# A dense weighted aggregation on TensorE: weight passes in one sweep on both column halves of the array, with four buffers of 3125 columns each loaded in one transfer

## The reference

```
x = _layernorm(x + _L2_gnn_ref(x, src, dst, edge_weight, gamma))

def hgcn_forward(x, rows, cols, edge_weight, gamma):     # rows = src, cols = dst
    h = x
    for _ in range(2):                                   # NUM_LAYERS
        msg = edge_weight[:, None] * h[cols]
        h = segment_sum(msg, rows, num_segments=6250)    # h = A h, A[row, col] = sum of weights
        h = proj(h)
        h = h * (1.0 / sqrt(|mink(h, h)|))
        h = lorentz_batchnorm(h, gamma)                  # means over all nodes, log map, exp map
    return h
```

## Time and profile before

| | |
|---|---|
| Runs | 7061.76, 7067.46, 7078.11 us; median 7067.46 |
| Profiled execution | 7070.5 us, of which the span (first to last record) is 7068.7 us |
| PE busy | 5556.2 us (79% of the span) |
| DVE / ACT / POOL busy | 3231.5 / 1350.6 / 2157.1 us |
| First weight pass | from 5516 to 6048 us |
| Second weight pass | from 6127 to 6659 us |

### The profile page before, as it was taken

The page is one execution under the profiler, slowest core; times in us unless marked ns, Lnnn a source line. Parts: engine busy times, 40 slices in busy tenths (PEclk is TensorE's granted clock), DMA queues, the critical chain, the costliest instruction groups (busy, mean ns, idle before and its releaser), DMA issues.

```text
span 7068.7 us, 161419 instructions
## 1 busy us (share of the span) xinstructions
PE 5556.2 (79%) x52264; PEld 4488.9 (64%) x52265; DVE 3231.5 (46%) x5888; ACT 1350.6 (19%) x3492; POOL 2157.1 (31%) x3521
## 2 busy tenths in 40 slices
PE   0999988877777779988377777777777899599765
PEld 0777777666666679988376777777666444244365
DVE  7999888777777740122333333333333100300233
ACT  0122234455555520000111111111111000100100
POOL 1222222222222210000377777777776000000000
PEclk9999999999999989998555555555565899799887
DMA  1011123334434339885533333333333799499565
GB/s 35 21 54 54 61 90 100 111 121 137 128 127 138 125 139 388 347 339 221 113 79 76 76 77 78 76 76 79 76 76 72 244 300 305 164 305 298 194 260 203
DMA packets 427400, 1053.65 MB, mean 149 GB/s; under 512 B 126711, under 2 KB 283713, under 8 KB 398401
## 3 DMA queue, kind: packets, MB, share of 16 engines
q1 hardware_dynamic: 377090, 1000.81, 42.4%
q0 software_dynamic: 50176, 51.48, 4.0%
HBM read 809.69 MB, written 242.41 MB: 149 GB/s over the span
## 4 chain that ended last, share of the span: by engine, by line
PE 49%; POOL 15%; DVE 14%; issue 10%; DMA 4%; ACT 3%; POOLq 2%; ACTq 2%; DVEq 0%; SPq 0%; PEldq 0%; PEld 0%
PE banks L1496 16%; POOL WORK L599 15%; PE banks L1526 15%; PE banks L1457 11%; PE banks L1488 4%; DVE T L803 3%; DMA WORK<-table,idx 3%; DVE T L810 2%; ACTq L332 1%; POOLq L336 1%; DVE WORK L879 1%; DVE WORK L892 1%; ACT WORK L1310 1%; DMA T<-qtable 1%; ACT ACC L1255 1%
## 5 line engine op out<-in xcount | busy, mean ns | idle before, releaser
L599 POOL DMA_INDIRECT WORK<-table,idx x1568 | 1525.9, 973 | 1372.1 <-DVE idx L898 894.3
L1496 PE MATMUL banks<-T 128*128 128x125 bf16 (+1 forms) x21696 | 1672.8, 226 | 41.4 <-DVE T L810 8.0
L1496 PEld LDWEIGHTS banks<-T 128*128 128x128 bf16 x21696 | 1446.4, 115 | 337.0 <-DVE T L810 321.3
L803 DVE TENSOR_TENSOR T<-T 128x750 bf16<-128x750 bf16 x1808 | 1001.6, 554 | 394.3 <-PE banks L1496 308.6
L556 POOL TENSOR_TENSOR T<-T 128x12 f32 x1816 | 551.0, 303 | 1785.1 <-DVE T L810 1289.7
L1526 PE MATMUL banks<-T,WORK 125*64 125x400 f32 (+1 forms) x3200 | 1056.6, 493 | 45.4 <-ACT WORK L1325 41.5
L810 DVE TENSOR_TENSOR T<-T 128x750 bf16<-128x750 bf16 x1808 | 1001.0, 554 | 62.1
L1488 PE MATMUL banks<-T 128*128 128x250 bf16 x3616 | 711.8, 278 | 364.4 <-DVE T L803 125.2
L1457 PE MATMUL banks<-WORK,T 125*128 125x192 bf16 (+1 forms) x10000 | 833.1, 247 | 63.1 <-DVE WORK L942 63.1
L1457 PEld LDWEIGHTS banks<-WORK,T 125*128 125x128 bf16 (+1 forms) x10000 | 830.9, 99 | 65.3 <-issue 59.3
L1526 PEld LDWEIGHTS banks<-T,WORK 125*64 125x64 f32 x3200 | 439.9, 138 | 661.5 <-issue 619.0
(11 more groups left out here) (337 smaller groups left out, 3428.1 us busy)
## 6 DMA issues: line engine op xcount, KB each, us to landing
T<-dense_c SPq DMA_DIRECT2D x200, 1562.5 KB, 8.3
T<-dense_w SPq DMA_DIRECT2D x300, 800.0 KB, 4.2
dense_w<-WORK SPq DMA_DIRECT2D x250, 546.9 KB
T<-dense_w SPq DMA_DIRECT2D x100, 725.0 KB, 4.1
WORK<-rel_rows SPq DMA_DIRECT2D x197, 256.0 KB, 4.0
WORK<-in_eaT SPq DMA_DIRECT2D x196, 256.0 KB
dense_c<-T SPq DMA_DIRECT2D x13, 3125.0 KB, 10.6
dense_c<-ACC SPq DMA_DIRECT2D x12, 3125.0 KB, 10.7
```

Of the source, the lines that this page charges most:

```text
L599: nc.gpsimd.indirect_dma_start(out=g_sb[:, u, c * D:(c + 1) * D], out_offset=None, in_=table, in_offset=bass.IndirectOffsetOnAxis(ap=idx[: ...
L803: V.tensor_tensor(planes[:, v, 0:HOTS].rearrange("p (k n t) -> p k n t", k=3, t=QUAD), iota2[:, 0:LO, :].unsqueeze(1).to_broadcast([P, 3, ...
L1496: last = T.matmul(banks[:, u, to - low // QUAD:to + LO + high // QUAD], keys[:, t, j, :], planes[:, v, first - low:past + high].rearrange( ...
```

## The change

A pass becomes one sweep over all 6250 columns. The columns are cut in two sides of SIDE = 3125. Side c = 0 goes to array columns and PSUM partitions 0 to 63, side c = 1 to 64 to 127 (`tile_position=(0, c * D)`). Both use the same `lt` tile and the same eight banks, now in pieces of 391 columns (the last of 388). The matmuls of the two sides alternate piece by piece.

Each side of a tile is one buffer, loaded in one transfer of 128 rows x 12500 bytes: side 0 and 1 of the even tile, side 0 and 1 of the odd tile. A buffer's `tile_used` comes at the end of its tile, for both sides together. The four buffers now fill T12 up to column 12500. So the loads of the first odd tile of a pass wait for the end of the chain before (`ln1 out`, `l2.0 out`). `ONES`, the row and the scalar values move to T1, and the ones of the last stage become `ONES3` where `ONES` was.

`ACC_full` takes both halves of the partitions (128 x 3125), one VectorE copy and two ScalarE copies a pass. 25 transposes of 128 x 125 follow, each with tile t of side 0 and tile t + 25 of side 1, and the copies to H scatter them (`H_sides`).

```diff
-SWEEP, PIECE = 3200, 400
+SIDE, PIECE = NODES // 2, 391
+HALF = 4 * PIECE
...
-        aw_sb = T12[:, 0:4 * 4 * PIECE].rearrange("p (s n) -> p s n", s=4)
+        aw_sb = T12[:, 0:4 * SIDE].rearrange("p (s n) -> p s n", s=4)
...
             for l in range(2):
-                for sw in range(2):
-                    with sp.Fori(0, NT // 2) as i:
-                        for u in range(4):
-                            first = sw * SWEEP + u % 2 * (4 * PIECE)
-                            past = min(NODES, first + 4 * PIECE)
-                            sp.wait_ge(tile_used, i * 4 + ((2 * l + sw) * 2 * NT + u + 1))
-                            sp.dma_start(aw_sb[:, u, 0:past - first], rows_of[ds(i * (2 * LO) + u // 2 * LO, P), first:past]).then_inc(tile_loaded[u], 16)
+                def side_in(i, y, c):
+                    sp.wait_ge(tile_used, i * 4 + (2 * l * NT + 2 * y + c + 1))
+                    sp.dma_start(aw_sb[:, 2 * y + c, :], rows_of[ds(i * (2 * LO) + y * LO, P), c * SIDE:(c + 1) * SIDE]).then_inc(tile_loaded[2 * y + c], 16)
+
+                side_in(0, 0, 0)
+                side_in(0, 0, 1)
+                sp.wait_ge(vector_done, v_order.at("l2.0 out" if l else "ln1 out"))
+                side_in(0, 1, 0)
+                side_in(0, 1, 1)
+                with sp.Fori(1, NT // 2) as i:
+                    for y in range(2):
+                        for c in range(2):
+                            side_in(i, y, c)
...
-                for sw in range(2):
-                    dve.wait_ge(tile_used, 4 + (2 * l + sw + 1) * 2 * NT)
-                    V.tensor_copy(ACC[:, sw * SWEEP:sw * SWEEP + 4 * PIECE].rearrange("p (j n) -> p j n", j=4), banks[0:D, 0:4, 0:PIECE]).then_inc(sweep_copied[0], 1)
+                dve.wait_ge(tile_used, 4 + (l + 1) * 2 * NT)
+                V.tensor_copy(ACC_full[:, 0:HALF].rearrange("p (j n) -> p j n", j=4), banks[:, 0:4, 0:PIECE]).then_inc(sweep_copied[0], 1)
...
             def dense_pass(l):
-                def tiles(sw, i, first):
-                    for u in range(4):
-                        if u % 2 == 0:
-                            pe.wait_ge(rows_taken, i * 2 + ((2 * l + sw) * NT + u // 2 + 1))
-                        pe.wait_ge(tile_loaded[u], i * 16 + ((2 * l + sw) * (NT // 2) + 1) * 16)
-                        for j in range(4):
-                            n = min(PIECE, NODES - sw * SWEEP - (u % 2 * 4 + j) * PIECE)
-                            last = T.matmul(banks[0:D, u % 2 * 4 + j, 0:n], lt[:, u // 2, :], aw_sb[0:LO, u, j * PIECE:j * PIECE + n],
-                                            start=first and u < 2, stop=False, skip_group_check=True)
-                        last.then_inc(tile_used, 1)
+                def tiles(i, first):
+                    for y in range(2):
+                        pe.wait_ge(rows_taken, i * 2 + (l * NT + y + 1))
+                        for c in range(2):
+                            pe.wait_ge(tile_loaded[2 * y + c], i * 16 + (l * (NT // 2) + 1) * 16)
+                        for j in range(8):
+                            n = min(PIECE, SIDE - j * PIECE)
+                            last = [T.matmul(banks[c * D:(c + 1) * D, j, 0:n], lt[:, y, :], aw_sb[0:LO, 2 * y + c, j * PIECE:j * PIECE + n],
+                                             start=first and y == 0, stop=False, skip_group_check=True, tile_position=(0, c * D)) for c in range(2)]
+                        for c in range(2):
+                            last[c].then_inc(tile_used, 1)
...
-                    for t in range(first, past):
-                        last = T.transpose(banks[0:LO, g, (t - first) * D:(t - first + 1) * D], ACC[:, t * LO:(t + 1) * LO], ident[0:D, 0:D])
+                    for t in range(4 * g, min(NT // 2, 4 * g + 4)):
+                        last = T.transpose(banks[0:LO, g, (t - 4 * g) * 2 * D:(t - 4 * g + 1) * 2 * D], ACC_full[:, t * LO:(t + 1) * LO], ident)
                     did(f"l2.{l} turned{g}", last)
```

More of the change, by code:

```diff
@@ L150, in gnn_kernel @@
         Y = H = by_node(WORK, 4800)
+        H_sides = H.rearrange("p (c t) f -> p c t f", c=2)
         XN, S2 = by_node(X_full, 0), by_node(X_full, NT * D)
@@ L164, in gnn_kernel @@
          n_u0, n_fac, n_clip, n_theta, n_exp, n_expm, n_sinhc, n_zc, n_poly, n_mask) = (T12[0:LO, 9600 + NT * i:9600 + NT * (i + 1)] for i in range(24))
-        ONES = T12[:, 10800:10800 + P]
-        r_part, r_mean, r_sq, r_mu, r_neg, r_nmu, r_std, r_gain = (T12[0:LO, 11000 + D * i:11000 + D * (i + 1)] for i in range(8))
-        s_space, s_mink, s_den, s_time, s_part, s_var, s_scale = (T12[0:LO, 11600 + i:11601 + i] for i in range(7))
+        ONES, ONES3 = T1_full[:, NT * D:NT * D + P], T12[:, 10800:10800 + P]
+        r_part, r_mean, r_sq, r_mu, r_neg, r_nmu, r_std, r_gain = (T1_full[0:LO, 3400 + D * i:3400 + D * (i + 1)] for i in range(8))
+        s_space, s_mink, s_den, s_time, s_part, s_var, s_scale = (T1_full[0:LO, 4000 + i:4001 + i] for i in range(7))
         dst_i = WORK[:, 0:COLS].bitcast(I32)
@@ L329, in tiles_of, with sides_of @@
             return banks[0:LO, bank, 0:(past - first) * D].rearrange("p (t f) -> p t f", f=D)
+        def sides_of(g):
+            n = min(NT // 2, 4 * g + 4) - 4 * g
+            return banks[0:LO, g, 0:n * 2 * D].rearrange("p (t c f) -> p c t f", c=2, f=D)
         def load(eng, of, low, high):
@@ L1065, in _ @@
                 pl = lambda name: p(f"l2.{l} {name}")
[L1066 to L1068 removed]
+                dve.wait_ge(tile_used, 4 + (l + 1) * 2 * NT)
+                V.tensor_copy(ACC_full[:, 0:HALF].rearrange("p (j n) -> p j n", j=4), banks[:, 0:4, 0:PIECE]).then_inc(sweep_copied[0], 1)
                 for g in range(0, len(EIGHT), 2):
                     pl(f"turned{g}")
[L1071 removed]
+                    did_l(f"moved{g}", V.tensor_copy(H_sides[:, :, 4 * g:min(NT // 2, 4 * g + 4), :], sides_of(g)))
                 al("squared")
@@ L1189, in _ @@
             plain_pass(3, 4, R, AGG)
-            did("ones again", V.memset(ONES, 1.0))
+            did("ones again", V.memset(ONES3, 1.0))
             did("self", V.tensor_tensor(HL, HL, of_nodes(dinv), ALU.mult))
@@ L1320, in _ @@
                 v("l2.0 out" if l else "ln1 out")
[L1321 to L1332, removed]
+                with act.Fori(0, NT // 2) as i:
+                    for y in range(2):
+                        act.wait_ge(tile_used, i * 4 + (2 * l * NT + 2 * y + 2))
+                        C.activation(lt[:, y, :], (H if l else XN)[:, ds(i * 2 + y, 1), :], ACT.Copy).then_inc(rows_taken, 1)
+                act.wait_ge(tile_used, 4 + (l + 1) * 2 * NT)
+                C.activation(ACC_full[:, HALF:HALF + 3 * PIECE].rearrange("p (j n) -> p j n", j=3), banks[:, 4:7, 0:PIECE], ACT.Copy)
+                C.activation(ACC_full[:, HALF + 3 * PIECE:SIDE], banks[:, 7, 0:SIDE - HALF - 3 * PIECE], ACT.Copy).then_inc(sweep_copied[1], 1)
                 for g in range(1, len(EIGHT), 2):
                     pl(f"turned{g}")
-                    did_l(f"moved{g}", C.activation(H[:, slice(*EIGHT[g]), :], tiles_of(g, *EIGHT[g]), ACT.Copy))
+                    did_l(f"moved{g}", C.activation(H_sides[:, :, 4 * g:min(NT // 2, 4 * g + 4), :], sides_of(g), ACT.Copy))
                 vl(f"moved{len(EIGHT) - 1}")
@@ L1518, in dense_pass @@
             def dense_pass(l):
-                def tiles(sw, i, first):
-                    for u in range(4):
-                        if u % 2 == 0:
-                            pe.wait_ge(rows_taken, i * 2 + ((2 * l + sw) * NT + u // 2 + 1))
-                        pe.wait_ge(tile_loaded[u], i * 16 + ((2 * l + sw) * (NT // 2) + 1) * 16)
-                        for j in range(4):
-                            n = min(PIECE, NODES - sw * SWEEP - (u % 2 * 4 + j) * PIECE)
-                            last = T.matmul(banks[0:D, u % 2 * 4 + j, 0:n], lt[:, u // 2, :], aw_sb[0:LO, u, j * PIECE:j * PIECE + n],
-                                            start=first and u < 2, stop=False, skip_group_check=True)
-                        last.then_inc(tile_used, 1)
[L1530 to L1536, removed]
+                def tiles(i, first):
+                    for y in range(2):
+                        pe.wait_ge(rows_taken, i * 2 + (l * NT + y + 1))
[7 more added lines that the diff above has]
+                            last[c].then_inc(tile_used, 1)
+                tiles(0, True)
+                with pe.Fori(1, NT // 2) as i:
+                    tiles(i, False)
             pe.wait_ge(edges_step, at_setup(0, "round_count"))
@@ L1646, in _ @@
                 for e in range(2):
-                    pe.wait_ge(sweep_copied[e], 2 * l + 2)
+                    pe.wait_ge(sweep_copied[e], l + 1)
                 for g, (first, past) in enumerate(EIGHT):
-                    for t in range(first, past):
-                        last = T.transpose(banks[0:LO, g, (t - first) * D:(t - first + 1) * D], ACC[:, t * LO:(t + 1) * LO], ident[0:D, 0:D])
```

(6 more changed lines are left out.)

## The result

The changed kernel takes 6878.4 us (median of 4 runs, 6870.3 to 6884.4) against 7064.9 before: 0.973 of the time, 95% interval 0.971 to 0.975, 187 us less. The forecast was 6810 in a range of 6745 to 6945, so the direction and the range held, and the gain is 71 us short of the 258 forecast. It also lies outside the forecast's own range (6755 to 6860): the range held because it took in the rival R2, at 27%.

What follows compares the result with a forecast made beforehand. TensorE was taken as the bound, then the loads at 8.1 us a tile: two passes, each 126.1 us shorter plus 2.7 for transposes, save 258 us from 7070.5, giving 6813, taken as 6810; range 6745 to 6945 (80%).

Steps and rivals of the forecast that it cites:

- R2: Rival for the weight passes: the halves overlap only in part, or the clock falls; 6860 to 6960 us, chance 27%.
- TensorE's work for a tile: Weight passes: the column halves work together, so a tile takes TensorE 5.7 us, between bounds of 5.25 and 10.5.
- R1: Rival for the weight passes: the halves do not overlap, a tile takes 10.5 us; 7040 to 7085 us, chance 12%.
- R3: Rival: weight loads no longer hide under matmuls, a tile takes 14.9 us; slower, up to 7490 us, chance 6%.
- first branch of R2: Each record waits for its 0.138 us of weights: 7.5 us of work, 9.0 us a tile, some 6900 us.
- The loads set the pace: Weight passes: TensorE goes from full to 70% busy; loads at 4.05 us each give 8.1 us a tile.
- The period, (tile + 0.3 + 10.1) / 2 = 8.05: Weight passes: time per tile from 5.7 us of work, 0.3 for semaphores and 10.1 for a pair's loads; 8.1 taken.
- I think the clock mostly holds: Weight passes: TensorE's clock stays near 1.00 though it idles 2.4 us of each 8.1, the work being dense.
- second branch: R2's other case: TensorE's clock falls because it idles 2.4 us of each 8.1; sign, a clock of 0.7.
- the forecast's own sign: Prediction is wrong in its size if the loads land further apart than 4.3 us or nearer than 3.8.
- The start of a pass: The second pair waits for "ln1 out" or "l2.0 out"; this new wait costs under 2 us, once a pass.
- The transposes: After each pass, 50 transposes in 8.05 us become 25 in 5.3 us, so 2.7 us less a pass.

Runs made afterwards that it cites:

- one_half: The changed kernel with both sides on array columns 0 to 63 in all tiles but the first: 7031.8 us, 0.997 of before.
- thin: The changed kernel with only the first of eight pieces computed in each tile but the first, all loads kept: 6727.5 us, 0.954 of before.
- three_pairs: The changed kernel with a third pair of buffers in NORM and a third slot for the tile of h: 6722.6 us, 0.953 of before.
- filler9: The changed kernel with 18 short f32 matmuls, results unread, before each tile's waits: 6866.8 us, 0.973 of before.
- quarters: The changed kernel with each side loaded in two transfers, released after four pieces each: 6743.8 us, 0.956 of before.
- in_turn: The changed kernel with eight matmuls of side 0 before the eight of side 1, side 0 released at its end: 6907.5 us, 0.979 of before.
- filler: The changed kernel with 12 short f32 matmuls, results unread, before each tile's waits: 6858.0 us, 0.973 of before.

## Why the prediction was right, and where it was short

*TensorE's work for a tile* (5.7 us forecast): right. It is 5.48 us at the full clock, 10.51 with one half, and no weight load came out of hiding, so R1, R3 and the first branch of R2 (7.5 us a tile) are out. No run shows the 5.7 itself, nor a tile of the 8.6 us at the far end of the forecast's own range: both were the author's estimates, and the runs showed 5.48 us of work and 8.87 a tile. The bounds of 5.25 and 10.5 can be had from the kernel before: its records of 400 columns start 0.3355 us apart, which is 0.328 for 391 in proportion, 16 or 32 of them a tile. one_half shows the upper one, 10.51 / 32 = 0.328 us a record, and the two halves gave 10.51 / 5.48 = 1.92 of 2. The loads of all records use the same rows, and one_half and the changed kernel both have them hidden: 0.14 us each (the 0.138 of the earlier trace rows is a mean, single ones take up to 0.23), one every 0.328 us on one half, two every 0.33 on both, with TensorE busy 400 of 400 us from 5550 to 5950 in one_half.

*The loads set the pace*: right in kind. The 4.05 us a load "with two in flight" was misread. The chain row has 2450 records, which are 49 blocks of 50, not 50 blocks, so 4.13 us a block, and TensorE is full there (20.00 of 20.00 us), so this is TensorE's pace and not the DMA engines'. With enough loads queued they give one in 3.77 (thin, three_pairs). The error hid behind the formula, which gave the same 8.1.

*The period, (tile + 0.3 + 10.1) / 2 = 8.05*: this is the step that failed, 8.87 us for 8.1, and with two terms. The first is the clock: "I think the clock mostly holds". It is 0.87 over 5600 to 5900, and the first tile of two takes 6.8 to 8.5 us. It was the author's estimate that it holds for dense work. The forecast took TensorE's idle time as 2.4 us after each tile. It had not seen that two slots released one after the other run into twos: one tile waits out the whole landing, the next is loaded by then, and the idle time falls into one gap of some 4.4 us, after which the clock is at 0.50. A slow first tile then lets most of the second pair's transfer pass under it (it lands at 5719.6, the tile ends at 5719.1), which keeps the gap together. The second is the 10.1 us of a landing. It holds for a pair issued when nothing is in flight, and it held in the even stretch of filler9, 7.9 us a tile. Over the whole passes of filler9, with the clock at 0.97, it is 11.4, and the period is 8.8 again. The 0.3 us for the semaphores was the author's estimate, and the trace bears it out: 0.13 us from the landing to the tile at 5712.23, 0.15 from its end to the issue at 5719.25. So the forecast's 8.1 needed the clock and the 10.1 us at once, and no run with two pairs released whole had both for long.

The result is where R2 has its second branch, the clock, at the near end of 6860 to 6960. The range was the author's estimate, with no term for this branch that a run shows; the runs showed a clock of 0.87 and 8.87 us a tile. The earlier trace rows were read as two stages with one busy share and no more. quarters and three_pairs show what was missing there: the same work in the same time keeps 1.00 in short pieces and 0.95 in longer ones. By the forecast's own sign it was wrong in its size: the loads land 8.87 / 2 = 4.4 us apart, and the sign was 4.3.

*In numbers*: 48 tiles x 0.77 us is 37 us a pass, the difference between 441.1 and the 404.0 forecast; two passes are 74, less the 2 us that the transposes gave beyond theirs, 72 for the 71 missed.

*The start of a pass*: right for the first, where TensorE waits 1.91 us for the second pair, for "under 2". In the second pass it waits 3.35 us, as the first tile takes 7.35 us there in place of 7.83:

```profile
6042.80 7.12 PE L1532 MATMUL banks<-T,WORK 125*64 125x391 f32 x32 [3.35 <-DMA T<-dense_w]
```

*The transposes*: 4.8 and 2.8 us, 2.7 forecast. The clock decides here: 25 transposes took 3.0 us at 1.00, 4.7 at 0.66 from 6475 to 6480, and the 25 with 125 columns 5.2 at 0.68.

## What to carry to other kernels

When a faster engine turns a stage over to its loads, work out the loop through a buffer, from issue to landing to release, and compare it with the transfer rate; with two slots the loop was longer here than the rate allows, and a third slot or an earlier release of parts took the difference (here 2% of the kernel, with 187 us won and 140 left lying). Ask how the new idle time is cut up as well as how large it is: here the clock fell after a gap of 4.4 us and held with gaps of 1.0. Before mending the slow clock itself, ask what the loop does without it; here it went no faster. Two column halves nearly doubled (1.92) the f32 matmuls of 64 outputs, with their instructions by turns.

## What the runs showed of the hardware

- f32 matmuls of 64 x 391 on two column halves, by turns, overlapped almost fully: 32 records in 5.48 us (the changed kernel) against 10.51 on one half (one_half).
- Issued in blocks of eight matmuls for each side, some 3.6 records at each change of side still overlapped (in_turn, 17.47 us for 64 records, where none overlapping would take 21.0).
- A load of 128 rows x 12500 bytes with none, or the last 0.3 us of one, in flight ahead of it landed after 6.2 to 6.3 us (and those issued at 5702.03 and 5719.25 in the changed kernel); with loads queued behind each other one landed each 3.77 us (thin, 425 GB/s), and the rate was 2% less with rows of 6250 bytes (quarters, 418 GB/s).
- Two such loads issued together with nothing in flight had both landed after 10.0 us (the changed kernel). Issued 2 to 4 us before the pair ahead had landed, they took 9.9 to 13.4 us (filler, filler9), so that a tile took 8.8 us at a clock of 0.97 where the queue kept full gave 7.5 (thin, three_pairs).
- TensorE's clock was 1.00 with 1.0 us idle after each 2.85 us of work (quarters), 0.95 with 2.0 idle after 5.5, with every fifth tile slow (three_pairs), and 0.87 with some 4.4 idle after 12.3 to 14 (the changed kernel).
